# A perceiver block on one Trainium2 core: the stage of the latents rebuilt

## The reference

```python
def xattn(x, latents, mask, ...):            # x = context, latents = _layernorm(x)
    xn, ln = _ln(x, g_x, b_x), _ln(latents, g_l, b_l)
    q = ln @ w_q
    k, v = split(concat([xn, ln], 1) @ w_kv)
    attn = softmax(mask(q * 64**-0.5 @ k.T))          # 8 heads of 64
    return _ln((attn @ v) @ w_out, g_o, b_o)
x = x + xattn(ctx_1024, _layernorm(x), mask, ...)
x = x + differential_attention(_layernorm(x), ...)    # 16 half heads of 32, rope
x = x + ffn_fp4(_layernorm(x), w_gate, w_up, w_down)  # weights and rows rounded to FP4 blocks
```

## Time and profile before

| | |
|---|---|
| median of 3 runs | 1122.6 us (1121.35 to 1122.88) |
| the profiled execution, its own time | 1121.62 us |
| its span, first to last instruction | 1119.7 us |
| mean granted TensorE clock | 0.976 of full speed |
| first scores of batch 0 | 133.6 us after the start of the span |

### The profile page before, as it was taken

The page is one execution under the profiler, slowest core; times in us unless marked ns, Lnnn a source line. Parts: engine busy times, 40 slices in busy tenths (PEclk is TensorE's granted clock), DMA queues, the critical chain, the costliest instruction groups (busy, mean ns, idle before and its releaser), DMA issues.

```text
span 1119.7 us, 16956 instructions
## 1 busy us (share of the span) xinstructions
PE 1011.0 (90%) x6468; PEld 788.7 (70%) x6468; DVE 810.1 (72%) x1857; ACT 451.3 (40%) x883; POOL 158.8 (14%) x176
## 2 busy tenths in 40 slices
PE   1698899999999999999999999889999879999996
PEld 1586688878788778788777887545555557777784
DVE  7734468798798897987988964255466478888873
ACT  3343346544654465446544653234343322222221
POOL 0332001121020211210212110022131100000000
PEclk9798899999999999999999999999999889999998
DMA  7478424144323442342244423070002150000000
GB/s 250 131 224 217 125 75 135 60 130 131 101 79 128 128 131 68 123 135 86 84 124 128 123 76 113 16 257 1 2 1 90 62 207 10 10 10 10 10 10 19
DMA packets 63184, 106.90 MB, mean 95 GB/s; under 512 B 30081, under 2 KB 34817, under 8 KB 60801
## 3 DMA queue, kind: packets, MB, share of 16 engines
q1 hardware_dynamic: 54528, 76.99, 21.5%
q0 software_dynamic: 8576, 28.84, 8.4%
HBM read 71.74 MB, written 34.08 MB: 95 GB/s over the span
## 4 chain that ended last, share of the span: by engine, by line
PE 57%; DVE 28%; ACT 6%; issue 5%; DMA 3%; POOL 1%; SPq 1%; DVEq 0%; ACTq 0%; POOLq 0%
PE ps_banks L138 12%; PE ps_banks L140 12%; PE ps_banks L139 12%; PE ps_banks L503 10%; PE ps_banks L394 7%; PE ps_banks L477 2%; DVE sb_b_stats L706 1%; DVE sb_eh_xn L863 1%; DVE sb_eh_amax L851 1%; DVE sb_ctx L719 1%; DVE sb_wq_big L883 1%; DMA scratch_q<-sb_a_q0lo 1%; DVE sb_w_q L891 1%; DVE sb_kT_lo L746 1%; DVE sb_hid_q L891 1%
## 5 line engine op out<-in xcount | busy, mean ns | idle before, releaser
L138 PE MATMUL ps_banks<-sb_zT_hi,sb_wkv_hi 128*128 128x512 f32 x256 | 106.2, 415 | 3.7 <-DVE sb_kT_lo L746 3.7
L138 PE MATMUL ps_banks<-sb_wkv_hi,sb_zT_hi 128*128 128x512 f32 x256 | 105.3, 411 | 0.0
L140 PE MATMUL ps_banks<-sb_wkv_hi,sb_zT_lo 128*128 128x512 f32 x256 | 100.7, 393 | 0.0
L140 PE MATMUL ps_banks<-sb_zT_hi,sb_wkv_lo 128*128 128x512 f32 x256 | 100.4, 392 | 0.0
L139 PE MATMUL ps_banks<-sb_wkv_lo,sb_zT_hi 128*128 128x512 f32 x256 | 100.1, 391 | 0.0
L139 PE MATMUL ps_banks<-sb_zT_lo,sb_wkv_hi 128*128 128x512 f32 x256 | 100.0, 390 | 0.0
L1213 ACT ACTIVATE sb_kT_hi<-ps_banks 128x512 fp32r<-128x512 f32 x64 | 38.0, 596 | 142.7 <-PE ps_banks L140 142.7
L138 PE MATMUL ps_banks<-sb_wgu,sb_z_hi 128*128 128x512 f32 (+1 forms) x192 | 74.6, 389 | 2.4 <-DVE sb_z_lo L746 2.4
L140 PE MATMUL ps_banks<-sb_wgu,sb_z_lo 128*128 128x512 f32 (+1 forms) x192 | 72.9, 380 | 0.0
L139 PE MATMUL ps_banks<-sb_wgu,sb_z_hi 128*128 128x512 f32 (+1 forms) x192 | 72.9, 380 | 0.0
L746 DVE TENSOR_TENSOR sb_zT_lo<-sb_zfull,sb_zT_hi 128x512 fp32r<-128x512 f32 x64 | 44.1, 690 | 30.5 <-ACT sb_zT_hi L1263 30.4
(11 more groups left out here) (236 smaller groups left out, 2524.1 us busy)
## 6 DMA issues: line engine op xcount, KB each, us to landing
sb_ctx<-in_ctx SPq DMA_DIRECT2D x16, 1024.0 KB, 5.6
sb_qpack<-scratch_q SPq DMA_DIRECT2D x16, 512.0 KB, 6.0
sb_wgu<-scratch_wgu SPq DMA_DIRECT2D x8, 1024.0 KB, 10.3
scratch_wgu<-sb_w_hi POOLq DMA_DIRECT2D x22, 256.0 KB, 3.2
scratch_wgu<-sb_w_lo POOLq DMA_DIRECT2D x22, 256.0 KB, 3.3
sb_wdn<-scratch_wdn SPq DMA_DIRECT2D x2, 2816.0 KB, 13.0
sb_wgu<-scratch_wgu SPq DMA_DIRECT2D x4, 768.0 KB, 13.9
sb_w_in<-in_w_gate SPq DMA_DIRECT2D x11, 256.0 KB, 2.7
```

Source lines behind the costliest of these rows:

```text
L138: e.matmul(o, wh, xh, start=i == 0, stop=False)
L140: m = e.matmul(o, wl, xh, start=False, stop=i == n - 1)
```

## The change

- **Norms.** The two norms of a latent row become one. If a row has variance v, the first norm leaves the variance v / (v + eps), so both together scale by the power -0.5 of (v + eps)(v / (v + eps) + eps) = v (1 + eps) + eps^2. `latent_stats` computes this `ve`, `norm_latents` applies it. The first half is handled in two parts of two tiles; the statistics of the second half stand behind the first `lo_of_latents`, its normalising behind the fourth.
- **Loads.** The first four tiles of x are loaded one by one, ahead of `ident`, `cols` and `w_q`. The small constants (`g_o`, `b_o`, `cosin`, `lnwb`, the lambdas) are loaded after the masks, and these wait for the latents alone.
- **First queries.** `first_queries` runs over the chunks of features outside and the four banks inside, so a chunk is multiplied as soon as its low part is there.
- **Order on PE.** The transposes of the second half stand together behind the four latent keys of the first half. `ring_a` hands out all eight banks in the first stage. The rings of the later blocks start at another bank, and the list of the third block is worked out from the banks held.
- **Staging.** Eight buffers `qk_stage` (one for each n of queries and of keys, used once a half) hold high and low part side by side, without zeros, and four `v_stage`. One transfer spills both parts (pieces of 512 B). `q_spill` has 64 columns. The zero halves are written once into `q_pack` by DVE (`zero_pack`), and `load_pack` reads q in two transfers of 64 partitions with pieces of 256 B.
- **Around the batches.** Pack 0 is loaded when the queries are spilled, ahead of the spills of the second half's keys and values. `normalise(0)` stands whole behind the low part of `w_out`. Zeroing of pack 1 and of the padding and the products of the lambdas stand in batch 0, slot 3; the first two FP4 weights are loaded after it; the rest of the lambdas' work stands in batches 1 and 2.

```diff
-        q_spill = scratch("q", [NB, P, C, 2, P], F32)
+        q_spill = scratch("q", [NB, P, C, 2, LQ], F32)
...
+        qk_stage = [sb(stage_a, f"a_qk{i}", [P, HALF // LQ, 2, LQ], F32R) for i in range(4)]
+        v_stage = [sb(stage_a, f"a_v{i}", [P, D]) for i in range(2)]
...
-                bank = claim(("lnT", half, c), Ring([c], uses, took))
+                bank = claim(("lnT", half, c), ring_a)
...
+            def first_queries():
+                on.wait_ge(w_lo_split, 1)
+                banks = [claim(("q", 0, n), ring_a) for n in range(C)]
+                for c in range(C):
+                    on.wait_ge(ln_lo_done, c + 1)
+                    for n, bank in enumerate(banks):
+                        cs = slice(n * P, (n + 1) * P)
+                        for i, (w, x) in enumerate(((wq_hi, ln_hi), (wq_hi, ln_lo), (wq_lo, ln_hi))):
+                            m = e.matmul(psum[:, bank, :], w[:, c, cs], x[0][:, c, :], start=c == 0 and i == 0, stop=c == C - 1 and i == 2)
+                        if c == C - 1:
+                            m.then_inc(filled[bank])
...
+                on.wait_ge(q_zeroed[i], 2)
+                on.wait_ge(pack_landed[i], 80 * (b // 2 + 1))
...
             for c in range(C):
                 turn_latents(0, c)
-            for n in range(C):
-                query(0, n)
+            first_queries()
             for n in range(C):
                 latent_key(0, n)
-                turn_latents(1, n)
+            for c in range(C):
+                turn_latents(1, c)
...
+            held = [took["gu", 0, 2, g][0] for g in range(2)]
+            ring.banks, ring.at = [0, 1] + [bank for bank in (3, 4, 5, 6, 7, 2) if bank not in held] + held, 0
...
+            def latent_stats(half, first, n):
+
+
+                stats, mv, ve, rstd = small_a[half]
+                for i in range(first, first + n):
+                    on.wait_ge(x_landed[4 if half else i], 16)
                     small_stats(x_row(half, i), i, small_a[half])
-                    yield
-                nth = finish_stats(0, 4, small_a[half])
-                yield
-                for i in range(4):
-                    normal(x_row(half, i), x_row(half, i), i, small_a[half], nth, x_first_normed)
-                    yield
-                for i in range(4):
-                    on.wait_ge(x_first_normed, 4 * (half + 1))
-                    small_stats(x_row(half, i), i, small_a[half])
-                    yield
-                nth = finish_stats(0, 4, small_a[half])
-                yield
-                for i in range(4):
+                for i in range(first, first + n):
+                    on.wait_ge(dve_chain.sem, dve_chain.value)
+                    e.bn_aggr(mv[:, i, :], stats[:, i, :]).then_inc(dve_chain.up())
+                on.wait_ge(dve_chain.sem, dve_chain.value)
+                e.tensor_scalar(ve[:, first:first + n], mv[:, first:first + n, 1], 1.0 + EPS_LN, EPS_LN * EPS_LN,
+                                ALU.mult, ALU.add).then_inc(rstds.up())
+                return rstds.value
...
+            def norm_latents(half, first, n, nth):
+                for i in range(first, first + n):
                     normal(x_row(half, i), x_row(half, i), i, small_a[half], nth, x_normed)
...
-                qh, ql = q_stage[slot]
-                on.wait_ge(q_hi_done, 2 * (C * half + n + 1))
-                for h, r in enumerate(HEAD_ROWS):
-                    e.scalar_tensor_tensor(
-                        out=ql[r, :, r], in0=blocks(psum[r, bank, :], LQ), scalar=DH ** -0.5,
-                        in1=qh[r, :, r].bitcast(F32), op0=ALU.mult, op1=ALU.subtract).then_inc(drained[bank] if h else dve_chain.up())
+                stage = qk_stage[staged(0, n)]
+                on.wait_ge(q_hi_done, C * half + n + 1)
+                e.scalar_tensor_tensor(out=stage[:, :, 1, :], in0=blocks(psum[:, bank, :], LQ), scalar=DH ** -0.5,
+                                       in1=stage[:, :, 0, :].bitcast(F32), op0=ALU.mult, op1=ALU.subtract).then_inc(drained[bank])
...
+            def zero_pack(i):
+                for h, r in enumerate(HEAD_ROWS):
+                    e.memset(q_pack[i][r, :, :, HEAD_ROWS[1 - h]].bitcast(U32), 0).then_inc(q_zeroed[i])
+                e.memset(vl_pack[i][LQ:P, :], 0.0).then_inc(b_zeroed)
...
             e.memset(half_pow[:, :], -0.5).then_inc(pow_set)
-            for i in range(2):
-                for part in range(2):
-                    e.memset(q_stage[i][part][:, :, :].bitcast(U32), 0).then_inc(q_zeroed)
-            first, second = norm_twice(0), norm_twice(1)
-            advance(first, 1000)
+            nth = [latent_stats(0, first, 2) for first in (0, 2)]
+            norm_latents(0, 0, 2, nth[0])
+            norm_latents(0, 2, 2, nth[1])
             split_lo(w_raw[:, :, :], wq_hi[:, :, :], wq_lo[:, :, :], w_hi_split, 1, w_lo_split)
-            for c in range(C):
+            lo_of_latents(0, 0)
+            nth = latent_stats(1, 0, 4)
+            for c in range(1, C):
                 lo_of_latents(0, c)
-                advance(second, 2)
+            norm_latents(1, 0, 4, nth)
             split_lo(wkv_raw[:, :, 0:D], wkv_hi[:, :, 0:D], wkv_lo[:, :, 0:D], w_hi_split, 2, w_lo_split)
             for n in range(C):
                 lo_of_query(0, n)
-                advance(second, 3)
             split_lo(wkv_raw[:, :, D:2 * D], wkv_hi[:, :, D:2 * D], wkv_lo[:, :, D:2 * D], w_hi_split, 3, w_lo_split)
             for n in range(C):
                 lo_of_latent_key(0, n)
-                advance(second, 1000)
+            for n in range(C):
                 lo_of_latents(1, n)
             split_lo(w_raw[:, :, :], w_out_hi[:, :, :], w_out_lo[:, :, :], w_hi_split, 4, w_lo_split)
-            norm = normalise(0)
+            on.wait_ge(ln_lo_done, 2 * C)
+            e.memset(mask_bias[:, :], 0.0).then_inc(b_zeroed)
+            advance(normalise(0), 1000)
             for n in range(C):
                 lo_of_query(1, n)
-                advance(norm, (0, 1, 2, 2)[n])
             for n in range(C):
                 lo_of_latent_key(1, n)
-                advance(norm, 4)
+            for i in (0, 2):
+                on.wait_ge(qk_spilled[i], 32)
+            zero_pack(0)
             for n in range(C):
                 taken(("q", 1, 3))
                 lo_of_z(0, n)
...
+                    if b == 0 and slot == 3:
+                        lam_products()
+                        for i in range(QK_BUFFERS):
+                            on.wait_ge(qk_spilled[i], 32 if i < C else 16)
+                        on.wait_ge(last_keys_spilled, 16 * C)
+                        for h in range(2):
+                            on.wait_ge(vl_spilled[h], 64)
+                        zero_pack(1)
+                        for i in range(2):
+                            e.memset(p_t[i][LQ:P, CS, :], 0.0).then_inc(p_zeroed)
+                    if b == 2 and slot == 2:
+                        lam_difference()
...
-                on.wait_ge(q_zeroed, 4)
-                if u >= 2:
-                    on.wait_ge(q_spilled[slot], 32 * (u // 2))
-                for r in HEAD_ROWS:
-                    e.activation(q_stage[slot][0][r, :, r], blocks(psum[r, bank, :], LQ), ACT.Copy, scale=DH ** -0.5).then_inc(q_hi_done)
+                if half:
+                    on.wait_ge(qk_spilled[i], 16)
+                e.activation(qk_stage[i][:, :, 0, :], blocks(psum[:, bank, :], LQ), ACT.Copy, scale=DH ** -0.5).then_inc(q_hi_done)
...
-            for half in range(2):
-                power(small_a[0][3][:, 0:4], small_a[0][2][:, 0:4]) if half == 0 else power(small_a[1][3][:, 0:4], small_a[1][2][:, 0:4])
-                if half == 0:
-                    power(small_a[0][3][:, 0:4], small_a[0][2][:, 0:4])
+            for first in (0, 2):
+                power(small_a[0][3][:, first:first + 2], small_a[0][2][:, first:first + 2])
+            power(small_a[1][3][:, :], small_a[1][2][:, :])
             for n in range(C):
                 spill_query(0, n)
-                if n == 1:
-                    power(small_a[1][3][:, 0:4], small_a[1][2][:, 0:4])
             for n in range(C):
                 spill_latent_key(0, n)
             for k in range(4):
                 spill_latent_value(0, k)
+            power(small_b[3][:, :], small_b[2][:, :])
             for n in range(C):
                 spill_query(1, n)
-            power(small_b[3][:, :], small_b[2][:, :])
...
             def load_pack(b):
                 i = b % 2
-                on.wait_ge(b_zeroed, 5)
                 if b >= 2:
                     on.wait_ge(v_weighed, C * (b - 1))
-                copy_bits(e, q_pack[i][:, :, :, :], q_spill[b]).then_inc(pack_landed[i], 16)
+                for r in HEAD_ROWS:
+                    copy_bits(e, q_pack[i][r, :, :, r], q_spill[b, r]).then_inc(pack_landed[i], 16)
...
+            for i in range(4):
```

(71 more changed lines are left out.)

108 lines of the change are left out of this document (47 added, 61 removed).

## The result

The changed kernel takes 1084.0 us (median of 4 runs, 1083.5 to 1085.73) where the kernel before took 1122.7 beside it: ratio 0.966, 95% interval 0.9643 to 0.9677. Forecast was 1085.5 within 1079 to 1094, faster. The profiled execution took 1083.58 us for a span of 1081.8.

The account below looks back on a forecast made before the run. It took PE, busy 90% of the span, as the bound, with gains only where PE idles or runs slowly before the first scores. Terms 15.5 + 7.4 + 7.8 + 5.2 + 2.0 - 1.1 = 36.8 us gave 1085.5 us, range 1079 to 1094.

Parts of the forecast that it names:

- The start: Up to the last first query: queries start at 15.5 us, ready at 28.3 instead of 43.78, 15.5 us saved.
- the slow stretch that I took over from the kernel before: First queries: PE runs chunk 0 at half clock at first, 4 us, then full speed, done at 20.2.
- w_q decides: Start: the landing of w_q, taken as 10.5 us within 9.3 to 11.8, sets when the first queries begin.
- Keys and transposes: Half 0's keys and half 1's transposes: 12.7 us instead of 20.07, 7.4 us saved.
- Values and context: Values and context transposes: context normed at 64, needed at 74.0; 12.7 us for 20.48, 7.8 saved.
- Pack 0: Before first scores: issued at 75, landed by 84 to 85, cover 13 us; 5.2 and 2.0 us saved.
- Added work: Batch 0, slot 3: DVE's lambda products and five memsets delay the transposes of context 1, 1.1 us lost.
- Pieces: Pack loads: 896 more pieces cost at most 10.7 us a batch, under 10.9 us of cover, so nothing lost.
- the rival of the pieces: Pack loads in the batches: pieces are the bound and each batch waits; 1125 to 1140 us, chance 0.04.
- my bound: Pack loads: 12 ns a piece, if all of a 6.1 us transfer were the cost of pieces.
- The sum: Whole kernel: savings less the loss make 36.8 us, from 1121.6 to 1084.8, predicted as 1085.5.

Follow-up runs that it names:

- after_again: The changed kernel run once more, unchanged, beside the others on the same chip: 1084.6 us, ratio 0.9671.
- twice_half0: The changed kernel with only half 0 of the latents normed twice again, half 1 once: 1086.3 us, ratio 0.9687.
- one_load: The changed kernel with the x tiles of half 0 loaded by one transfer instead of four: 1082.8 us, ratio 0.9657.
- no_chunk: The changed kernel with the first queries column block by column block again, each over all four chunks: 1090.0 us, ratio 0.9718.
- by_chunk: The changed kernel with w_q loaded, copied and split in four chunks, VectorE's start reordered, batch 0's products and clearings behind slot 4: 1079.7 us, ratio 0.9621.
- interleaved: The changed kernel with each group of half 1's transposes behind a key of half 0, as before the change: 1085.1 us, ratio 0.9673.
- four_undone: The changed kernel with latents normed twice, first queries by column blocks, two staging buffers a kind, and masks, constants, pack 0 behind the last spills: 1104.8 us.
- two_buffers: The changed kernel with two staging buffers each for queries and keys instead of four, half 1's keys spilled by POOL: 1096.3 us, ratio 0.9774.
- pack_last: The changed kernel with masks, constants and pack 0 issued behind the last spills, as before: 1091.3 us, ratio 0.9727.
- pieces64: The changed kernel with each pack's queries loaded in pieces of 64 B instead of 256 B, eight transfers for two: 1083.5 us, ratio 0.966.
- twice: The changed kernel with the latents normed twice again, in both halves: 1092.9 us, ratio 0.9743.
- reordered: The changed kernel with half 1's statistics behind chunk 1's low part and batch 0's products and clearings behind slot 4: 1082.8 us, ratio 0.9656.

## Why the prediction was right, step by step

- **The start.** Queries done at 28.55 for 28.3: 15.2 us saved for 15.5. That it came out so near is luck, two errors that cancel. w_q was copied from 11.28 for 10.5, so the first query came at 16.3 for 15.5; and the slow stretch that I took over from the kernel before did not come, so chunk 0 took 3.0 us and ran into low part 1, 0.95 us late. With the slow stretch (after_again) the queries end at 28.69 all the same: the stretch then lies where the hole was. The share of half 0's single norm is about 2.5 us (twice_half0), less than its 6.7 us of work, since w_q covers the rest; loading by tile gave nothing (one_load); the chunks gave 6 us (no_chunk). The prediction's sentence that w_q decides is what by_chunk shows: with w_q in chunks the first query comes 3.2 us earlier.
- **Keys and transposes.** 12.65 us for 12.7. Which part of the change brings the 7.4 depends on the rest. PE's order makes no difference while all else is changed (interleaved). The buffers make none here when PE comes late: four_undone runs this stage in 12.5 with two buffers and two norms. Of the change it keeps VectorE's order, in which half 1 is normed whole ahead of w_k's low part, and also PE's order and the eight banks. I hold the first to be the cause, as the hole before was a wait for the normed half 1, but no run undoes it.
- **Values and context.** 12.78 us for 12.7; the context is normed at 64.1 for 64. No run puts back the old place of `normalise(0)`, so its share of the 7.7 is not shown apart from the buffers' (two_buffers has a hole of 2.84 us here).
- **Pack 0.** Issued at 75.26 for 75, and PE doesn't wait. Its last load lands at 77.92 + 2.9 = 80.8 us, where I had 84 to 85, so the cover up to the scores at 97.56 was 16.7 us for my 13. In pack_last the same load is issued 19.8 us later and takes 5.3 us instead of 2.9, and PE waits 4.5 us for it. The 7.3 us of that run are not the pack's alone: PE is 1.1 us late ahead of the wait (98.65 for 97.56), because its first queries ran at half clock for longer.
- **Added work.** The hole in batch 0 is 1.16 us for 1.1, with VectorE's two products and five clearings from 96.28 to 98.6 ahead of the context's normalising. It costs no slow stretch.
- **Pieces.** No wait on a pack in any batch, so the rival of the pieces is out: pieces64 has four times as many, and its price of 1 ns is a twelfth of my bound.
- **The sum.** Worked with the measured terms: 43.78 - 28.55 = 15.2, 20.07 - 12.65 = 7.4, 32.99 - 32.65 = 0.3, 20.48 - 12.78 = 7.7, 11.0 - 10.9 = 0.1, the hole of 5.2 and its slow stretch of 1.95, less 1.16: 36.8 us, as predicted. Some cuts of the earlier trace rows lie 0.2 us ahead of the next step (the first key comes at 44.01, not 43.78), which moves 0.2 us from one term to another and leaves the sum. The lead read at PE's landmarks is 36.5, and the 37.9 us between the two spans has 1.4 more. Of this 1.7 arise from a stretch at half clock that the trace of before has behind a hole of 2.55 us in the third block, and the trace of after doesn't have behind the same hole of 2.53 us; 0.3 are lost again behind it. The windows behind that hole, first before, then after:

```profile
745.70:747.70 2.00, 2.00 (x4) 0.96 (x4) 0.00 (x0) 0.60 (x1) 0.00 (x0) 0.50 0.44 154
747.70:749.70 2.00, 2.00 (x4) 0.74 (x4) 0.00 (x0) 0.00 (x0) 0.00 (x0) 0.76 0.02 8
```

```profile
708.50:710.50 2.00, 2.00 (x8) 1.24 (x9) 0.39 (x1) 0.60 (x1) 0.00 (x0) 1.00 0.76 269
```

I don't count this as a gain of the change: of the 14 profiles taken here 7 have the stretch and 7 have not, though the changed kernel and its variants differ in nothing there (without it also after_again, twice, twice_half0, no_chunk, two_buffers, one_load; with it also interleaved, reordered, by_chunk, pieces64, pack_last, four_undone). That it is chance from one execution to the next is not shown: after_again was to show it and lacks the stretch again. So 36.5 of the 37.9 us belong to the first stage and batch 0, and the other 1.4 come from a place that no term of the prediction names.

What stays open: four_undone is still 17.2 us faster than the kernel before. Its trace puts this at the end of the queries (39.2 for 44.0), at the keys and transposes (12.5 for 20.0) and at the values and the context (15.6 for 20.6). VectorE's orders, PE's order, the eight banks, the loads by tile, the earlier loads of the context, and the halved bytes of the queries with one transfer a spill are what remains changed. Of these only PE's order and the loads by tile were undone alone; the others were not run apart from each other.

## What to carry to other kernels

Take the stage's full-clock length per matmul from a stage without holes, and price every other stage as what it exceeds that by; then follow each engine's order to see whether the cover holds. Parts that remove waits on the same path don't add up: here they were worth 34.5 us one by one and 20.8 together, because when one goes, its neighbour's delay becomes visible. Look for the load that decides the start before shortening the chain beside it: here that was w_q, and cutting it in chunks brought the next 3.9 us.

## What the runs showed of the hardware

The column of the granted clock says 1.00 also where the trace has no record of the clock yet, and the first record comes between 12 and 32 us. The windows of the first 12 query matmuls of pack_last (first record at 21.15) and, for comparison, of 18 later ones:

```profile
16.19:21.03 4.84, 4.84 (x12) 3.79 (x13) 4.34 (x11) 2.17 (x4) 1.38 (x1) 1.00 0.78 269
22.01:26.09 4.08, 4.08 (x19) 3.38 (x18) 4.08 (x6) 1.43 (x1) 0.00 (x0) 1.00 0.00 0
```

Both rows say 1.00, but a matmul takes 0.43 us in the first and 0.23 in the second. So the first queries of pack_last ran at half clock, as did those of four_undone up to its first record at 31.36 and those of pieces64 up to 18.55. The 1.00 of the changed kernel's first row holds, as its first record is at 14.59 and its steps are 0.23.

A short hole of PE doesn't settle whether PE is granted 2.4 or 1.2 GHz behind it. Between the first transposes and 140 us PE ran at full clock behind holes of 1.56 (interleaved), 2.25 (the changed kernel) and 2.51 us (four_undone), and at half clock behind 1.66 and 2.12 (before), 1.90 (reordered), 2.73 (after_again), 2.84 and 3.00 us (two_buffers). Behind each of the nine longer ones, of 4.19 to 7.63 us, it ran at half clock. Such a stretch costs about 1.7 us (after_again) to 2.8 us (no_chunk, four_undone) at the first queries, which take 10.9 at full clock, and I had charged the one at the start as certain. The page "TensorE: Matmul & The Clock Gate" of the Trainium skill, section "Part 1: The HAM clock gate (the "warmup" mystery)", says that the number of slow matmuls varies from run to run of one kernel with the phase at its start; the two profiles of the changed kernel agree, with no first query at half clock in one and 8 in the other.

Loads in short pieces cost less than my bound: each 128 KB of the queries in pieces of 256 B landed in 5.9 us (median), where 512 KB in pieces of 4 KB had taken 6.0, and pieces of 64 B added 1 ns each. What grew was SyncE's time to issue: 1.21 us for two transfers, 6.29 for eight.
